# Two units per query half: a new order of the attention units, and the feed-forward part of the last four-tile group begun earlier

## What is computed

```
x = x + attention(layernorm(x))            # 16 heads of 64, 4 x 1024 tokens
    q, k, v = x @ Wq.T, x @ Wk.T, x @ Wv.T
    sim = einsum('bhid,bhjd->bhij', q, k) * 64 ** -0.5
    e = exp(sim - max(sim)); attn = e / (sum(e) + 1e-10)
    out = einsum('bhij,bhjd->bhid', attn, v) @ Wo.T + bo
x = x + ffn(layernorm(x))
    fp4_linear(h, w) = quant(h) @ quant(w).T   # blocks of 16, 8 levels of size
    gate, y = fp4_linear(x, w_gate), fp4_linear(x, w_up)      # 352 wide
    out = fp4_linear(silu(gate) * y, w_down)
```

## Time and profile before

| what | us |
|---|---|
| median of three runs | 1541.71 |
| the profiled execution, its own time | 1543.96 |
| its span, first to last instruction | 1542.1 |
| PE busy in the span | 1462.9 |
| POOL busy | 1247.5 |
| DVE busy | 1177.7 |
| ACT busy | 1129.8 |

### The profile page before, as it was taken

The page is one execution under the profiler, slowest core; times in us unless marked ns, Lnnn a source line. Parts: engine busy times, 40 slices in busy tenths (PEclk is TensorE's granted clock), DMA queues, the critical chain, the costliest instruction groups (busy, mean ns, idle before and its releaser), DMA issues.

```text
span 1542.1 us, 35223 instructions
## 1 busy us (share of the span) xinstructions
PE 1462.9 (95%) x13828; PEld 968.6 (63%) x13828; DVE 1177.7 (76%) x2048; ACT 1129.8 (73%) x2082; POOL 1247.5 (81%) x1358
## 2 busy tenths in 40 slices
PE   4999999999999999999999999999999999999965
PEld 2566666666666666666666666666666666666644
DVE  7777787777777878687787868788686877868677
ACT  3777777777777777777777777777777777777732
POOL 4888989878888888788888878888888888878952
PEclk9999999999999999999999999999999999999997
DMA  6111110101111111111111111101111111111000
GB/s 166 43 42 43 42 43 22 43 22 42 43 42 43 31 36 26 42 43 46 36 32 25 43 43 42 46 23 37 30 46 43 42 36 31 26 42 45 3 4 14
DMA packets 46661, 59.78 MB, mean 39 GB/s; under 512 B 8672, under 2 KB 21920, under 8 KB 46496
## 3 DMA queue, kind: packets, MB, share of 16 engines
q1 hardware_dynamic: 46336, 57.26, 15.8%
q10 hardware_dynamic: 160, 0.26, 0.1%
HBM read 4.80 MB, written 2.10 MB: 4 GB/s over the span
## 4 chain that ended last, share of the span: by engine, by line
PE 76%; DVE 17%; POOL 3%; ACT 2%; issue 1%; DMA 1%; SPq 0%; ACTq 0%; DVEq 0%
PE ob L621 24%; PE st L593 14%; PE st L595 11%; PE sm L574 9%; DVE negm L905 6%; PE mb L510 5%; PE mb L526 4%; PE mb L515 2%; POOL p_low L437 2%; PE mb L1177 2%; DVE xn L1151 2%; PE mb L521 1%; DVE qw L1069 1%; PE mb L1188 1%; PE mb L539 1%
## 5 line engine op out<-in xcount | busy, mean ns | idle before, releaser
L437 POOL TENSOR_TENSOR p_low<-probs 128x512 f16<-128x512 f32 x1024 | 1081.5, 1067 | 234.1 <-ACT probs L720 228.4
L720 ACT ACTIVATE probs<-st,lift,exp_scale 128x512 f32<-128x512 f32 x1024 | 793.0, 775 | 236.7 <-PE st L595 213.2
L905 DVE TENSOR_REDUCE negm<-sm 128x1 f32<-128x1024 f32 x508 | 617.8, 1216 | 130.4 <-PE sm L574 128.2
L593 PE MATMUL st<-q_hl,k_hh 128*128 128x512 f16 x1024 | 394.0, 385 | 2.3 <-DMA q_hm<-m_low 2.3
L595 PE MATMUL st<-q_hm,k_l 128*128 128x512 f16 x1024 | 388.7, 380 | 0.0
L621 PEld LDWEIGHTS ob<-v,p_low 128*128 128x128 f16 x4096 | 274.4, 97 | 123.0 <-POOL p_low L437 2.9
L621 PEld LDWEIGHTS ob<-v,probs 128*128 128x128 bf16 x4096 | 275.4, 97 | 120.7 <-ACT probs L720 0.5
L621 PE MATMUL ob<-v,p_low 128*128 128x129 f16 x4096 | 315.7, 219 | 2.7 <-POOL p_low L437 2.7
L621 PE MATMUL ob<-v,probs 128*128 128x129 f16 x4096 | 316.7, 219 | 0.2
L574 PE MATMUL sm<-k_hh,q_hl 64*128 64x512 f16 x508 | 196.9, 388 | 25.2 <-DVE negm L905 22.3
L574 PE MATMUL sm<-k_hh,q_hm 64*128 64x512 f16 x508 | 197.0, 388 | 0.0
(11 more groups left out here) (169 smaller groups left out, 1541.7 us busy)
## 6 DMA issues: line engine op xcount, KB each, us to landing
k_hh<-k_high SPq DMA_DIRECT2D x128, 128.0 KB, 2.3
k_l<-k_low SPq DMA_DIRECT2D x64, 128.0 KB, 2.3
q_hl<-q_high SPq DMA_DIRECT2D x64, 128.0 KB, 2.3
q_hl<-q_low SPq DMA_DIRECT2D x64, 128.0 KB, 2.4
q_hm<-q_high SPq DMA_DIRECT2D x62, 128.0 KB, 2.3
x<-x SPq DMA_DIRECT2D x4, 512.0 KB, 7.2
q_hm<-m_high SPq DMA_DIRECT2D x128, 1.0 KB
q_hm<-m_low SPq DMA_DIRECT2D x128, 1.0 KB
```

The costliest lines, as they stand in the source:

```text
L437: return pool.tensor_tensor(p_low[b][:, j, :], p, p.bitcast(BF16)[:, 1::2], ALU.subtract)
L593: pe.matmul(st[s % 2][:, :], k_hh[n][:, s * P:(s + 1) * P], q_hl[n][:, half * HALF:(half + 1) * HALF], start=True, stop=False)
L720: nc.scalar.activation(probs[k % 2][:, s, :], st[s % 2][:, :], ACT.Exp, bias=lift[:, 0:1], scale=exp_scale[:, head, pair:pair + 1]).then_i ...
L905: nc.vector.tensor_reduce(negm[k % 2][:, s // 2:s // 2 + 1], banks[:, :, :].rearrange("p a n -> p (a n)"), AX.X, ALU.max, negate=True).the ...
```

## The change

The units of a round now go half by half: head 0 half 0, head 1 half 0, head 0 half 1, head 1 half 1. Both heads of tiles 0 to 3 are thus complete after two units, and t0 of a pair moves from (0, 7) of the next round to (3, 5) of its own. Its output product o0 stays at (1, 3) of the next round; for the last pair alone a new job e0 does it at (3, 7) of round 32. Behind that, the feed-forward part of the last batch's first four tiles begins: statistics in slot (3, 7) of round 32 on DVE, the root on POOL in the same slot ahead of the last p_low, norm and quantising of x at places of round 33, its transposes on PE and its first gate and up products there too. The quantising of hidden of the last two early tiles, all but whose first steps stood in round 33, goes to (3, 3) to (3, 6) of round 32 (LATE_H). Behind round 33 the order of the late groups is x0, hidden 0, x1, hidden 1, 2, 3, where it was x0, x1, hidden 0 to 3.

```
-        ("q0", 0, (0, 5), (0, 6), (0, 6)), ("t0", 0, (0, 7), (1, 0), None), ("m", 0, (1, 1), (1, 2), (1, 2)),
+        ("q0", 0, (0, 5), (0, 6), (0, 6)), ("m", 0, (1, 1), (1, 2), (1, 2)),
...
-        ("u1", 1, (3, 1), None, (3, 2)), ("m", 1, (3, 3), (3, 4), (3, 4)), ("n1", 0, (3, 3), (3, 4), (3, 4))]
+        ("u1", 1, (3, 1), None, (3, 2)), ("m", 1, (3, 3), (3, 4), (3, 4)), ("n1", 0, (3, 3), (3, 4), (3, 4)),
+        ("t0", 0, (3, 5), (3, 6), None), ("e0", 0, (3, 7), None, (3, 7))]
...
+LATE_H = ((3, 3), (3, 4), (3, 4), (3, 5), (3, 6), (3, 6))
+LATE_X = ((0, 0), (0, 2), (0, 6), (0, 7), (1, 3))
...
-    if name in "to":
-        return prev
+    if name == "t":
+        return cur if JOBS[n][0] == "t0" else prev
+    if name == "o":
+        return prev and (JOBS[n][0] == "o1" or nxt or cur)
+    if name == "e":
+        return r == NPAIR
...
-            return 2 * (4 * (g - 1) + k - back) + bank, pq, pk // 2, (pk % 2) * IT + 2 * bank
+            return 2 * (4 * (g - 1) + k - back) + bank, pq, pk % 2, (pk // 2) * IT + 2 * bank
...
-                    head, half = (k + 1) // 2 % 2, (k + 1) % 2
+                    head, half = (k + 1) % 2, (k + 1) % 4 // 2
...
+                            if r == NPAIR and (k, s) == (3, SLOTS - 1):
+                                ffn.late_root(pool, 0)
                             low_part(k % 2, s).then_inc(s_lp, 1)
...
-                    wait(pe, s_on, 8 * (g - 1) - 2 * (1 - c))
+                    wait(pe, s_on, 8 * (g - 1) + 4 * (1 - c))
                     for t in range(4):
-                        last = pe.transpose(bank[:, t * P:(t + 1) * P], o_n[1 - q][:, 4 * c + t, :], ident[:, :])
-                elif name[0] == "o":
-
-                    wait(pe, s_ot, 2 * (g - 2) + c + 1)
+                        last = pe.transpose(bank[:, t * P:(t + 1) * P], o_n[1 - q if c else q][:, 4 * c + t, :], ident[:, :])
+                elif name[0] in "oe":
+
+                    pair = g - 2 if name[0] == "o" else g - 1
+                    wait(pe, s_ot, 2 * pair + c + 1)
...
-                    head, half = k // 2, k % 2
+                    head, half = k % 2, k // 2
...
-                        n = 2 * q + 1 if k < 2 else 2 * (1 - q)
-                        h = n % 2
-                        if k % 2 == 0 and s == 1:
-                            wait(pe, s_dkh[h], 32 * (g + (1 if k else 0)))
-                            wait(pe, s_dqh[h], 32 * (g + (1 if k else 0)))
+                        n = 2 * q + k if k < 2 else 2 * (1 - q) + k - 2
+                        if k >= 2 and s == 1:
+                            wait(pe, s_dkh[n % 2], 32 * (g + 1))
...
-                            pq, ph = (1 - q, 1) if k == 0 else (q, (k - 1) // 2)
+                            pq, ph = (1 - q, 1) if k == 0 else (q, (k - 1) % 2)
...
+                        if r == NPAIR + 1 and (k, s) == (1, 5):
+                            ffn.turn_late(pe, ident, 0)
+                        if r == NPAIR + 1 and (k, s) == (1, 7):
+                            ffn.gate_up(pe, 0)
...
+                        if r == NPAIR + 1 and (k, s) == (1, 6):
+                            ffn.copy_late(act, 0)
+                        if r == NPAIR + 1 and (k, s) == (2, 0):
+                            ffn.tanh(act, 0)
...
+                        if r == NPAIR and (k, s) == (3, 7):
+
+                            dve.wait_ge(s_x2, 2 * NPAIR - 1)
+                            ffn.late_stats(dve, x2, 0)
                         if r == NPAIR + 1:
-
-                            if (k, s) == (1, 5):
-                                dve.wait_ge(s_x2, 2 * NPAIR - 1)
-                                ffn.late_stats(dve, x2, 0)
-                            if (k, s) == (2, 1):
+                            if (k, s) == (0, 0):
+
+                                dve.wait_ge(s_pv, 8 * NPAIR - 2)
+                                ffn.late_norm(dve, x2, 0)
+                            for part, place in enumerate(LATE_X):
+                                if (k, s) == place:
+                                    ffn.late_x(dve, 0, part)
+                            if (k, s) == (2, 0):
                                 dve.wait_ge(s_x2, 2 * NPAIR)
                                 ffn.late_stats(dve, x2, 1)
 
-                                dve.wait_ge(s_pv, 8 * NPAIR)
-                                ffn.late_x(dve, x2, 0)
-                            if (k, s) == (3, 1):
-                                ffn.late_x(dve, x2, 1)
...
+LATE_ORDER = (("x", 0), ("h", 0), ("x", 1), ("h", 1), ("h", 2), ("h", 3))
...
-            for part, place in enumerate(AT_H_BEGIN):
+            for part, place in enumerate(AT_H_BEGIN if n < TWOS - 1 else LATE_H):
...
-        if n is not None:
+        if n is not None and n < TWOS - 1:
...
-        root(0)
-        root(1)
         self.end(pool, 0)
+        gate(0)
+        self.late_root(pool, 1)
+        gate(1)
         self.end(pool, 1)
-        gate(0)
-        gate(1)
-        for i in range(self.LATE - 1):
-            self.end(pool, 2 + i)
-            if i + 2 < self.LATE:
-                gate(i + 2)
+        self.end(pool, 2)
+        gate(2)
+        self.end(pool, 3)
+        gate(3)
+        self.end(pool, 4)
...
+        self.gate_up(pe, 1)
+        down(0)
+        self.turn_late(pe, ident, 1)
+        self.gate_up(pe, 2)
+        down(1)
+        self.gate_up(pe, 3)
+        down(2)
+        down(3)
...
+        self.tanh(act, 1)
+        hidden_turned(0)
+        self.copy_late(act, 1)
+        self.tanh(act, 2)
+        hidden_turned(1)
+        self.tanh(act, 3)
+        hidden_turned(2)
+        hidden_turned(3)
...
+        hidden(0)
+        self.late_norm(dve, x2, 1)
+        self.late_x(dve, 1, ALL_BUT_LAST)
+        hidden(1)
+        add(0)
+        hidden(2)
+        add(1)
+        hidden(3)
+
+        dve.wait_ge(self.s_lq, 5)
+        self.end(dve, 5)
+        add(2)
+        add(3)
 
```

132 lines of the change are left out of this document (60 added, 72 removed).

## The result

The changed kernel takes 1558.2 us (median of four executions, 1555.0 to 1563.6) against 1542.4 for the kernel before on the same chip: ratio 1.0105, 95% interval 1.0088 to 1.0121. It is slower, as forecast, but by 15.8 us where I had 6.7, and above the range. One execution in the experiments, the profiled one of f5, ran at a granted clock of 0.65 and took 2081 us; it is left out of f5's time, and f5 has no trace to set beside the others.

What follows compares the result with a forecast made beforehand. PE alone was taken to bound even rounds, with DVE adding 1.28 us in odd ones. Body +5.7 and end +1.0 made +6.7 us, 1548.4 us against the 1541.71 median; range 1542.5 to 1553.5.

Steps and rivals of the forecast that it cites:

- t0 leaves (0, 7): Body: removing t0's 0.44 us there gains 0 in eleven odd rounds; PE's wait before (1, 1) grows to 0.56 us.
- the body's 5.7: Up to unit 2 of round 32: t0's move loses 0.44 us in 13 rounds, +5.7 us in sum.
- The contention at (3, 2): DVE and POOL meet there, PE may wait 0.66 us at (3, 5); -2.6 to +4.6 us possible, no change taken.
- rival 3: The coin of (3, 2) falls against PE in all eleven odd rounds: +4.6 us, 1553.0; chance 0.14.
- The order of heads: Body: the new order adds and removes no instruction, head 1's scores come long after their transfers; cost 0.
- The end of round 32: Sums of (3, 5) to 1474.3, e0's addition 1477.8, last p_low 1481.7; last low products start 5.0 us later.
- rival 2: End: x0's whole chain leaves it, 4.3 us shorter, if e0's addition comes before 1475.4 in old time; 1537.4 with body 0; chance 0.08.
- the price of the root ahead of p_low: End of round 32: the last unit's low products start 5.0 us later because POOL's root precedes the last p_low.
- The seven steps of LATE_H: End of round 32: DVE's seven quantising steps beside busy POOL take 6.05 us, to 1473.9 in old time.
- First hidden product 3.5 us earlier: Round 33: through the same links plus 1 us, the first hidden product begins at about 1498.0, 3.5 us earlier.
- From there to the end 42.8 us: First hidden product to last addition: old 38.35 us, plus x1's 6.4, less waits of about 1.9.
- up to +4: End's upper bound: PE at slower clock in the links and third group's gate late, down of hidden 1 ahead of fourth gate and up.

Runs made afterwards that it cites:

- f5: Changed kernel with the (3, 2) quantising step at (2, 7), x1 ahead of the first hidden product, gate_up(3) ahead of down(1): 1550.5 us, ratio 1.0052.
- f6: Changed kernel with DVE's (3, 2) step at (2, 7) and hidden quantising steps at (0, 0), (0, 3), (1, 0), (1, 2), (1, 4): 1541.0 us, ratio 0.9992.
- f7: Kernel before, t0 kept at (0, 7), with the same DVE quantising places as f6: 1532.0 us, ratio 0.9938.
- e2: Kernel before with the new order of units and t0 moved to (3, 5), old tail kept: 1548.1 us, ratio 1.0037.
- e1: Kernel before with only the new order of units, t0 and tail as before: 1541.6 us, ratio 0.9998.
- f1: Changed kernel with one number changed, DVE's quantising step of (3, 2) moved to (2, 7): 1556.5 us, ratio 1.0074.
- e3: Changed kernel with t0 back at (0, 7) for every pair but the last, new tail kept: 1549.2 us, ratio 1.0050.
- f3: f1 with the root of the first four tiles on POOL behind the last p_low instead of ahead: 1555.4 us, ratio 1.0068.
- f2: f1 with gate_up(3) ahead of down(1), its tanh earlier on ACT and add(1) inside DVE's last quantising: 1552.4 us, ratio 1.0045.
- e4: Kernel before with two DVE quantising steps moved, (3, 2) to (2, 7) and (0, 4) to (0, 3): 1540.5 us, ratio 0.9992.
- g5: Changed kernel with e3's t0, f6's places, f2's and f3's orders, LATE_H behind x0, x1 first, x0's norm behind sums, o1 first: 1530.7 us, ratio 0.9914.

## Why the prediction was right in sign and wrong in size

- **t0 leaves (0, 7), gain 0 in odd rounds: right.** The wait at (1, 1) is 0.56 us as forecast, in eleven rounds, and f6 and f7 show the reason. In round 8 it cost 0.4 too. Round 5 was mis-sized: 0.44 became 1.26, by a step of DVE that grew from 0.18 to 0.90 us beside POOL. With it the body's 5.7 is 6.5 us (e2 less e1). By the traces t0 costs 7.0 us up to the last scores, 0.44 of it at (3, 5) of round 32, which the 5.7 left out.
- **The contention at (3, 2), taken as unchanged: wrong.** This is rival 3. In the profiled execution it took ten of eleven rounds, 6 x 0.67 = 4.0 us more than in the trace before, and at the median 1.7 us, or 4.8 by the ratios (f1). The failure was to take one trace's four rounds as the kernel's property, "as the same slots precede it": kernels with the same neighbours had it in 0 (e1, e3), 1 (e2), 4 and 10 rounds. Which way it fell in the changed kernel was luck; that it could fall so was in the rival, at 0.14.
- **The order of heads, cost 0: right** (e1).
- **The end of round 32: right, and it did not matter.** The sums end at 1485.7; less 11.0 (the distance of the last regular hidden product in the two traces) that is 1474.7, forecast 1474.3; e0's addition ends at 1478.6, forecast 1477.8, so rival 2, which needed it before 1475.4, was out; the last p_low 1482.5, forecast 1481.7. I called the 5 us "the price of the root ahead of p_low"; f3 gave back 4.4 of it for 0.6 at the end. The seven steps of LATE_H took 6.5 us where I had 6.05. It is too much to say that each DVE step waits beside a busy POOL: the first, a reduction, took 0.89 us there, as long as in the tail with POOL idle, and the second took 0.90 instead of 0.19.
- **First hidden product 3.5 us earlier: it was 1.2.** x0 was quantised 1.2 us later than forecast, and the links after it took 10.6 us from its end (1500.62 to 1511.23) instead of 9.7.
- **From there to the end 42.8 us: this term failed.** It was 48.4 (1511.23 to 1559.61). I had taken the old waits off and put no new ones in, and there were 6.9 us of them. The order of down(1) and gate_up(3) stood in the bounds ("up to +4") and not in the sum; it is worth 6.0 us in the trace, 4.1 at the median (f2), and with f2's edit the stretch lasts 43.1 us, as forecast. The tail costs 7.6 us (e3 less e1), or 8.4 between the traces of before and after, where the sum had 1.0.
- **The granted clock** is lower in the longer tail: 0.72 against 0.82, and PE is busy for 45.8 us in it against 40.0. f2 shows that the missing 5.6 us do not come from it, as its clock is no higher. Of the rest of the tail's loss no run says how much is the clock's.
- **The range** took either the worst end (+4) or rival 3, not both. Both came, and the end went beyond +4.

At the medians, 6.5 for t0 and 7.6 for the tail make 14.1 of the 15.8 us; the remaining 1.7 lie within what f1 gives for the contention. Between the two traces it is 7.0 for t0, 4.4 for six more rounds of contention and 8.4 for the tail: 19.8 us. That the forecast of a small loss had the right sign is owed to the body; the tail alone had been forecast within noise of no change, and it lost more than t0 did.

## What to carry to other kernels

Work taken off the busiest engine ahead of a point where it waits is worth nothing; move first what makes the other engine late (f6). If the wait only moves to the next such point, look at the lengths of the other engine's steps: one that starts earlier can meet a third engine's step and give the gain back (e4). When streams are written out by hand for several engines, follow each engine's wait to what stands ahead of the releasing instruction in the releaser's own queue: an independent product behind a waiting one was the dearest item of the tail here (f2). Starting a chain early gains only what its later joins let through, so sum the tail by the engine that is full in it. A kernel that beats both needs four places in two lists of DVE's steps changed (f7, 0.9938); the early start on top of it gives 0.9914 (g5), with intervals that overlap.

## What was not expected of the hardware

One nanosecond in the distance of two starts decides 0.9 us. In the traces of the kernel before, the changed one and e1 to e3, POOL's p_low starts ahead of the DVE step of the earlier trace rows in all 55 odd rounds from 11 on, by 26 to 34 ns. At 31 ns or less (31 rounds) the DVE step is free: it takes 0.27 us, and p_low 1.20. At 33 or 34 ns (11 rounds) it is held: it takes 1.15 us and p_low 1.04, and the step ends 0.15 us after p_low. At 32 ns both occur, 9 times free and 4 times held. So it can fall differently from round to round within one execution. The Trainium skill (SBUF — State Buffer, section Who interferes with whom) says that whoever issues first holds the shared pair for its whole instruction. The traces agree that one is held by the other, and show that the order of the starts in a profile doesn't tell which: POOL's start is first in all 55. The distance nearly does. What happens at that moment no trace here shows.

In round 5 a step of 24 columns went from 0.18 to 0.90 us in the same way, since it started while p_low ran. So a short step costs nearly as much as a long one there (0.72 us more, against 0.88): what it pays is set by how much of POOL's step is left. e4 has such a loss too, of 0.76 us in every odd round looked at, on a step whose place the edit had not touched.
